# A state-space block rebuilt chunk by chunk ahead of a six-layer attention stack

## What is computed

```python
h = _layernorm(x) * (1 + ca) + sa                     # ca, sa, ga from silu(c) @ wmod
x1 = h * rsqrt(mean(h * h) + EPS) * norm_w
skip = x1 @ skip_w.T                                  # 128 -> E = 256
u = silu(causal_conv(x1 @ in_w.T, conv_w) + conv_b)   # 4 taps, per channel
delta = softplus(u @ Wd1.T @ Wd2_w.T + Wd2_b)
Bm, Cm = u @ WB.T, u @ WC.T                           # N = 16 states
# scan over positions, for each of 256 channels and 16 states:
#   H = exp(delta * A) * H + delta * u * B ;  y = sum_n H * C
y = (y + u * W_D) * silu(skip)
x = x + ga * (h + y @ out_w.T)
h2 = _layernorm(x) * (1 + cb) + sb                    # goes into the attention stack
x = x + gb * six_layers(h2)                           # q,k,v projection, rotary tables, windows of 32, FFN
```

## Time and profile before

| | us |
|---|---|
| median of 3 runs | 2322.53 (2317.49 to 2326.46) |
| the profiled execution | 2319.96 |
| its span, first to last instruction | 2318.0 |
| PE busy | 1991.3 (86%) |
| DVE busy | 1698.9 (73%) |
| ACT busy | 1470.9 (63%) |
| POOL busy | 1239.8 (53%) |

### The profile page before, as it was taken

One profiled execution on the slowest core, in us unless ns is written; L12 is line 12 of the kernel. 1 busy time (PEld: TensorE's weight loads), 2 busy tenths in 40 slices (PEclk: granted clock), 3 DMA queues, 4 the chain that ended last, 5 costly groups with the idle time before them and its releaser, 6 DMA issues. The chain is left out here.

```text
span 2318.0 us, 85232 instructions
## 1 busy us (share of the span) xinstructions
PE 1991.3 (86%) x32884; PEld 1450.5 (63%) x32884; DVE 1698.9 (73%) x3114; ACT 1470.9 (63%) x4554; POOL 1239.8 (53%) x1362
## 2 busy tenths in 40 slices
PE   4546566499989999999999999999999999999997
PEld 2212122398677697676876867857769768687672
DVE  6579897598587696775876867858669677686673
ACT  2443232397677696676767867767669667686772
POOL 3046664576475375574554854647537557455450
PEclk7779899699999999999999999999999999999998
DMA  1022120411112111121111221111211111111110
GB/s 35 3 81 72 63 72 0 146 41 41 32 42 72 38 42 37 36 79 31 43 37 31 51 70 36 40 32 42 71 38 42 37 36 43 32 44 29 25 31 18
DMA packets 147573, 103.90 MB, mean 45 GB/s; under 512 B 15778, under 2 KB 140256, under 8 KB 145504
## 3 DMA queue, kind: packets, MB, share of 16 engines
q1 hardware_dynamic: 147184, 98.55, 15.3%
HBM read 47.79 MB, written 1.18 MB: 21 GB/s over the span
## 5 line engine op out<-in xcount | busy, mean ns | idle before, releaser
L947 ACT ACTIVATE PR<-ps,MN 128x64 f32<-128x64 f32 x1536 | 354.9, 313 | 389.3 <-DVE MN L1069 388.8
L1198 POOL TENSOR_TENSOR QK<-PC,PS 128x256 f32<-128x256 f32 x384 | 278.6, 725 | 600.1 <-DVE PS L1108 543.0
L1203 POOL TENSOR_TENSOR QK<-QK,RN 128x512 f32<-128x512 f32 x384 | 401.6, 1046 | 161.1 <-ACT RN L937 133.0
L821 PE MATMUL ps<-W,XS 128*128 128x256 f32 x1536 | 399.3, 383 | 19.2 <-DMA W<-in_Wqkv 18.9
L793 PE MATMUL ps<-V,PT 64*32 64x65 f32 x12288 | 301.7, 220 | 8.6 <-ACT PT L988 5.1
L821 PEld LDWEIGHTS ps<-W,XS 128*128 128x128 f32 x1536 | 264.4, 192 | 41.4 <-DMA W<-in_Wqkv 20.5
L807 PE MATMUL ps<-ident,QK 128*128 128x128 f32 x1536 | 253.2, 287 | 35.8 <-POOL QK L1203 33.5
L1199 POOL TENSOR_TENSOR QK<-PC,PS 128x256 f32<-128x256 f32 x384 | 278.9, 726 | 0.0
L1092 DVE TENSOR_REDUCE SS<-SQ 128x8 f32<-128x512 f32 x384 | 259.3, 675 | 16.4 <-ACT SQ L979 16.4
L793 PEld LDWEIGHTS ps<-V,PT 64*32 64x32 f32 x12288 | 257.4, 105 | 18.7 <-ACT PT L988 9.2
L1069 DVE TENSOR_REDUCE MN<-ps 128x4 f32<-128x256 f32 x384 | 161.1, 419 | 142.2 <-PE ps L774 140.0
(11 more groups left out here) (142 smaller groups left out, 3447.4 us busy)
## 6 DMA issues: line engine op xcount, KB each, us to landing
V<-V SPq DMA_DIRECT2D x384, 97.5 KB, 2.2
scr<-B_rows SPq DMA_DIRECT2D x32, 512.0 KB, 3.6
V<-V SPq DMA_DIRECT2D x288, 32.5 KB, 1.9
W<-in_Wqkv SPq DMA_DIRECT2D x48, 192.0 KB, 2.9
TC<-in_tcos SPq DMA_DIRECT2D x6, 1024.0 KB, 5.9
TS<-in_tsin SPq DMA_DIRECT2D x6, 1024.0 KB, 8.4
WO<-in_Wo SPq DMA_DIRECT2D x6, 512.0 KB, 4.7
W<-in_W SPq DMA_DIRECT2D x6, 341.0 KB, 3.4
```

What stands on the lines that cost most here:

```text
L821: mm = nc.tensor.matmul(ps[:, par, k * 2 * P:(k + 1) * 2 * P], cols[k], W[:, i, 0:2, :].rearrange("p t m -> p (t m)"), start=True, stop=True)
L947: e = nc.scalar.activation(PR[:, m % 2, h, slot * DH:(slot + 1) * DH], ps[:, 4 + h, slot * DH:(slot + 1) * DH], ACT.Exp, scale=-1.0, bias= ...
L1198: nc.gpsimd.tensor_tensor(QK[:, par, :, 0:hd], PC[:, par, :, 0:hd], PS[:, par, :, hd:DH], ALU.add)
L1203: nc.gpsimd.tensor_tensor(QK[:, par, :, :], QK[:, par, :, :], bcast_last(RN[:, par, :], DH), ALU.mult).then_inc(qk, 1)
```

## The change

Nothing of the arithmetic of the attention stack changes. In `mamba_block`:
- x comes in four DMAs, the weights behind three semaphores. The stages are interleaved by chunk in an order written out by hand in every stream.
- Each inverse root is exp(-0.5 * ln(v)) on ACT (`inverse`, `level`) in place of a square root on ACT and a reciprocal on DVE. Table sets are loaded by hand: six loads (silu, exp and ln, in turn).
- The convolution is folded into the input projection: POOL multiplies the input weights by the norm weights and by each tap (`w_tap`), and PE adds up four fp32 matmuls with `XN` shifted by the tap. 32 matmuls of 512 columns take the place of 8, and the 16 DVE steps are gone. The silu takes its input from PSUM.
- The joint projection's output is copied once, 96 rows (`MID`). The C row is spread by two fp32 matmuls whose stationary operand is one column of `ident`, repeated; `BCS`, `SEL` and their DVE and POOL work are gone. In PE's stream `spread(n+1)` stands between the two halves of `state(n)`, in place of after them; the loop over n is written out.
- Exp and ln of the softplus go over 1024 columns at a time; U is POOL's.
- The gates of batch 0 stand between drives of batch 1. Output projection, residual and second norm go chunk by chunk; the residual goes straight to `XRES`, the modulation writes `XS` directly (ACT the upper half, POOL the lower).
- Tables, the first layer's `W`, scales and mask are loaded in the first block: the tables and `W` (3.5 MB) on SP behind the second `spill` and ahead of the fetches of n = 4 and on. POOL scales the tables in 16 pieces between drives of batch 1; `transformer_block` starts without them.

Its core:

```diff
+            def spill(b):
+                sp.wait_ge(mid, 2 * b + 2)
+                half = slice(b * L, (b + 1) * L)
+                sp.dma_start(B_rows[:, half], MID[DDELTA:DDELTA + N, half]).then_inc(b_out[b], 16)
+
+            spill(0)
+            sp.wait_ge(b_out[0], 16)
             for n in range(4):
                 fetch(0, n, n)
+            spill(1)
+            sp.wait_ge(b_out[1], 16)
+            sp.dma_start(TC[0][:], d["tcos"]).then_inc(ld_tab, 16)
+            sp.dma_start(TS[0][:], d["tsin"]).then_inc(ld_tab, 16)
+            for t in range(3):
+                sp.dma_start(W[:, :, t, :], d["Wqkv"][0, :, t * INNER:(t + 1) * INNER]
+                             .rearrange("p (i m) -> p i m", i=PAIRS)).then_inc(ld_w0, 16)
...
+            def conv(c, h, bank):
+                pe.wait_ge(xn, c + 1)
+                for tap in range(DCONV):
+                    mm = nc.tensor.matmul(ps[:, bank, :], w_tap[:, tap, h * P:(h + 1) * P], xn_cols(c, tap),
+                                          start=(tap == 0), stop=(tap == DCONV - 1))
+                mm.then_inc(conv_ps, 1)
+
+            def skips(c, h, bank):
+                nc.tensor.matmul(ps[:, bank, :], w_skip[:, h * P:(h + 1) * P], xn_cols(c),
+                                 start=True, stop=True).then_inc(skip_ps, 1)
...
                                       start=True, stop=True)
             mm.then_inc(s_mod, 1)
-            pe.wait_ge(s_const, 1)
-            layer_norm(s_xt, mean_ps, cen, sq, var_ps, std)
-
+            for c in range(2):
+                var(c)
+                turn(c + 2)
+                mean(c + 2)
+                square(c)
+            var(2)
+            pe.wait_ge(s_taps, 2)
             pe.wait_ge(s_mod_sb, 1)
-            for c in range(NCH):
-                wait(pe, r_sq, c + 1)
...
+            conv(0, 0, 6)
+            square(2)
+            var(3)
+            conv(0, 1, 7)
+            square(3)
+            pe.wait_ge(s_xt, NCH)
+            conv(1, 0, 0)
+            conv(1, 1, 1)
+            pe.wait_ge(cen, NCH)
+            pe.wait_ge(ld_w, 80)
+            cat(0, 2)
+            pe.wait_ge(lnv, NCH)
+            skips(0, 0, 3)
+            skips(0, 1, 4)
+            pe.wait_ge(r_ln, NCH)
+            cat(1, 5)
+            skips(1, 0, 6)
+            skips(1, 1, 7)
+            rate(0, 0, 0)
+            rate(0, 1, 1)
+            pe.wait_ge(skip, 1)
+            conv(2, 0, 2)
+            conv(2, 1, 3)
+            pe.wait_ge(skip, 2)
+            rate(1, 0, 4)
+            rate(1, 1, 5)
+            pe.wait_ge(skip, 4)
+            conv(3, 0, 6)
+            conv(3, 1, 7)
+            pe.wait_ge(sp_abs, 2)
+            pe.wait_ge(relu_d, 2)
+            cat(2, 0)
+            skips(2, 0, 1)
+            skips(2, 1, 2)
+            cat(3, 3)
...
+            def spread(b, n):
+                wait(pe, hc, (b * N + n) * HALVES)
+                row = ident[DDELTA:DDELTA + 2 * N, DDELTA + N + n:DDELTA + N + n + 1].to_broadcast([2 * N, P])
                 for k in range(2):
-                    mm = nc.tensor.matmul(ps[:, bank + k, :], SEL[:, row, :],
-                                          BCS[:, b * L + k * CH:b * L + (k + 1) * CH], start=True, stop=True)
-                return mm
-
-            def state(b, n, first=False, last=False):
-                wait(pe, hc, (b * N + n) * HALVES)
-                spread(n + N, 2, b).then_inc(c_ps, 1)
...
-                        wait(pe, y_d, b * HALVES)
-                    for k in range(2):
-                        mm = nc.tensor.matmul(ps[:, 4 + 2 * h + k, :], ident[:], HC[h][:, k * CH:(k + 1) * CH],
-                                              start=first, stop=last, skip_group_check=True)
-                    mm.then_inc(yacc, 1)
-
-            pe.wait_ge(lo, 1)
...
+            def state(b, n, h, first=False, last=False):
+                pe.wait_ge(hc, (b * N + n) * HALVES + h + 1)
+                if first:
+                    wait(pe, y_d, b * HALVES)
+                for k in range(2):
+                    mm = nc.tensor.matmul(ps[:, 4 + 2 * h + k, :], ident[:], HC[h][:, k * CH:(k + 1) * CH],
+                                          start=first, stop=last, skip_group_check=True)
+                mm.then_inc(yacc, 1)
+
             pe.wait_ge(sp_abs, NCH * HALVES)
             pe.wait_ge(relu_d, NCH * HALVES)
+            pe.wait_ge(xc, 2 * NCH)
+            spread(0, 0)
...
+            def inverse(c):
+                act.wait_ge(var_ps, c + 1)
+                nc.scalar.activation(RST[:, c, :], ps[:, 4, :], ACT.Ln, bias=epsc[:]).then_inc(lnv, 1)
+                act.wait_ge(lnv, c + 1)
+                nc.scalar.activation(RST[:, c, :], RST[:, c, :], ACT.Exp, scale=-0.5).then_inc(rstd, 1)
...
+            def soft(c, banks):
+                for h in range(HALVES):
+                    n = 2 * c + h
+                    act.wait_ge(dl_ps, n + 1)
+                    nc.scalar.activation(SOFT[:, n, :], ps[:, banks[h], :], ACT.Abs,
+                                         bias=cols[:, h, 1:2]).then_inc(sp_abs, 1)
+                act.wait_ge(sp_abs, 2 * c + 2)
+                both = SOFT[:, 2 * c:2 * c + 2, :]
+                nc.scalar.activation(both, both, ACT.Exp, scale=-1.0).then_inc(sp_exp, 1)
+                act.wait_ge(sp_exp, c + 1)
+                nc.scalar.activation(both, both, ACT.Ln, bias=1.0).then_inc(sp_ln, 1)
+
...
-                c, k = q // 4, q % 4
-                act.wait_ge(pj_ps, q + 1)
-                if k < 2:
-                    dst = XP[:, k, c // 2, DCONV - 1 + (c % 2) * CH:DCONV - 1 + (c % 2 + 1) * CH]
-                    nc.scalar.copy(dst, ps[:, q % 8, :]).then_inc(pj, 1)
-                else:
-                    nc.scalar.activation(chunk(SK[:, k - 2, :], c), ps[:, q % 8, :], ACT.Silu).then_inc(pj, 1)
-            for n in range(HALVES * B):
-                h, b = n % 2, n // 2
-                act.wait_ge(conv, HALVES * B * (DCONV - 1) + n + 1)
-                v = XC[:, h, b * L:(b + 1) * L]
-                nc.scalar.activation(v, v, ACT.Silu).then_inc(xc, 1)
+            deviation(0)
+            for c in range(NCH):
+                inverse(c)
...
-
+            def centre(c):
+                dve.wait_ge(mean_ps, c + 1)
+                nc.vector.tensor_tensor(CEN[:, c, :], chunk(XT, c), ps[:, 2 + c % 2, :], ALU.subtract).then_inc(cen, 1)
+
+            def scaled(c):
+                dve.wait_ge(rstd, c + 1)
+                dve.wait_ge(sq, c + 1)
+                nc.vector.tensor_tensor(CEN[:, c, :], CEN[:, c, :], RST[:, c, :], ALU.mult).then_inc(z, 1)
...
+            def normed(c):
+                dve.wait_ge(r_rstd, c + 1)
+                dve.wait_ge(hh, c + 1)
+                nc.vector.tensor_tensor(xn_cols(c), chunk(H1, c), RMS[:, c, :], ALU.mult).then_inc(xn, 1)
...
+            pool.wait_ge(s_fold, 1)
+            pool.wait_ge(s_pads, 2)
+            nc.gpsimd.tensor_tensor(w_tap[:], w_tap[:], w_in[:].unsqueeze(1).to_broadcast([P, DCONV, E]),
+                                    ALU.mult).then_inc(s_taps, 1)
```

More of the change, by code:

```diff
@@ new lines, in silu, with gate_in, middle @@
+            def silu(c, h, bank):
+                act.wait_ge(conv_ps, 2 * c + h + 1)
+                nc.scalar.activation(chunk(XC[:, h, :], c), ps[:, bank, :], ACT.Silu,
+                                     bias=cols[:, h, 0:1]).then_inc(xc, 1)
+            def gate_in(c, h, bank):
+                act.wait_ge(skip_ps, 2 * c + h + 1)
+                nc.scalar.activation(chunk(SK[:, h, :], c), ps[:, bank, :], ACT.Silu).then_inc(skip, 1)
+            def middle(c, bank):
+                act.wait_ge(cat_ps, c + 1)
+                nc.scalar.copy(chunk(MID, c), ps[0:DDELTA + 2 * N, bank, :]).then_inc(mid, 1)
@@ new lines, in _ @@
+            soft(0, (0, 1))
+            soft(1, (4, 5))
+            load_set(nc, act, SILU)
+            for h in range(HALVES):
+                silu(2, h, 2 + h)
+            for h in range(HALVES):
+                silu(3, h, 6 + h)
+            middle(2, 0)
+            gate_in(2, 0, 1)
+            gate_in(2, 1, 2)
+            middle(3, 3)
+            gate_in(3, 0, 4)
+            gate_in(3, 1, 5)
+            load_set(nc, act, EXP_LN)
+            soft(2, (6, 7))
+            soft(3, (4, 5))
@@ L496, in _, with residual @@
                                                    ALU.mult, ALU.add).then_inc(y_d, 1)
-            for c in range(NCH):
+            def residual(c):
                 dve.wait_ge(o_ps, c + 1)
@@ new lines, in _ @@
+            for c in range(2):
+                for h in range(HALVES):
+                    drives(c, h)
+            pool.wait_ge(u_done, 2 * HALVES)
+            for k in range(4):
+                for h in range(HALVES):
+                    drive(0, 0, k, h)
+                    if k >= 2:
+                        drives(k, h)
+            with pool.Fori(1, N // 4) as m:
+                for k in range(4):
+                    for h in range(HALVES):
```

(13 more changed lines are left out.)

620 lines of the change are left out of this document (322 added, 298 removed).

## The result

The median fell from 2320.01 us (2315.67 to 2326.46) to 2236.5 us (2234.25 to 2243.84): a ratio of 0.9643, 95% interval 0.9627 to 0.9659, 83.5 us less. The forecast was 2239 in a range of 2230 to 2260.

The account below looks back on a forecast made before the run. PE was taken to bound everything from 436 us on, a chain of work with no engine full except DVE in the scan before that; 43.4 + 3.7 + 22.2 + 14.4 = 83.7 us off gave 2239, range 2230 to 2260.

Parts of the forecast that it names:

- the scan: Scans of both batches: period stays 7.26 us, the spread at 0.43 an instruction ending 0.4 us before it is wanted.
- The way to the first scan: Kernel start to first scan: 93.1 us against 136.55, 43.4 gained; 89.3 at full clock, 105 at half clock with PE bubbles.
- square(3): Last chunk's square in the first norms: ends on PE at 39.7 us at full clock, about 47 at half; 43.5 taken.
- PE's stream: After the norms, before the first scan: 48 matmuls without a long wait, 41.1 us at full clock.
- the end chain: From the last skip matmul's landing to the first scan: gate silu, table load, softplus steps and decay, 11.6 us not hidden.
- Rival 1: Way to the first scan: PE doesn't get its matmuls done in time, first scan at 105, total 2251 us; chance 0.17.
- rival 3: Scans: PE becomes the bound through half clock or slower spread instructions, 95 us over 32 states, total 2334; chance 0.03.
- Between the batches: Change of batch: scan no longer waits for POOL's gates, second D step 1.7 us later; 3.7 us gained, bounds 1 to 5.4.
- The tail: Last scan's end to the end of the first block's work: 26.5 us against 48.7, 22.2 gained; bounds 25.5 and 32.
- The seam: Start of the attention stack: 9.5 us from W already loaded, 4.9 from tables already scaled, 14.4 gained; bounds 9.5 and 15.
- Rival 2: Attention stack's start: only the load is gained, 6 of the 14.4 us go; total 2247 with tail losses; chance 0.08.
- rival 4: Scan at n = 4: the prefetch on SP delays it; 10 us beyond the 27 us cover gives 2249; chance 0.03.

Follow-up runs that it names:

- undo_seam: Changed kernel with the tables and first layer's W loaded and scaled in the attention block again: 2251.41 us, ratio 0.9702 to the kernel before.
- two_taps: Changed kernel with two of the convolution's four taps left out: 2224.81 us, ratio 0.9584 to the kernel before.
- loads4: Changed kernel with four more table loads ahead of the third chunk's softplus: 2245.15 us, ratio 0.9661 to the kernel before.
- spread96: Changed kernel with the C row spread from all 96 rows instead of 32, in the same four instructions: 2230.09 us, ratio 0.9604 to the kernel before.
- best: Changed kernel with the 96-row spread, and batch 0's last half-1 additions ahead of batch 1's first spread: 2230.48 us, ratio 0.9595 to the kernel before.
- scale2: Changed kernel with loads kept early but POOL scaling the tables at the attention stack's start: 2242.19 us, ratio 0.9655 to the kernel before.

## Why the prediction was right

The time was right and most of its steps were; one term, the scan, was sized at nothing and costs 3 to 6 us. It is also the sign that the prediction had named for being wrong: waits of DVE for PE in the scan.

- **The way to the first scan** (43.4 of gain forecast): 42.9 in the profile, 45.0 and 43.3 in the other two. The parts: `square(3)` done at 43.6 (43.5 said), PE's stream 42.4 us (41.1 said) at full clock from 45 us on, the end chain as walked (11.3 for 11.6). The 43.5 was chosen between 39.7 and 47 for an unknown clock, and these two don't add up from the prediction's own prices: three chunks at 5.9 make 39.1 with no room for the `conv` of 3.4 between them. So that it was hit is partly luck. The clock in the norms is the likely cause of the difference from the bound: in the profile of `undo_seam`, whose way is the same, the first 45 us were granted 1.00, `square(3)` was done at 38.9 and the first scan started at 88.9, near the bound of 89.3 for full clock; at 0.92 to 0.96 the other profiles with this way have 91.2 to 94.1, though not in the order of their clocks. That PE bounds the stream, `two_taps` shows; that it isn't by much, too. Rival 1, half clock and PE bubbles up to 105, didn't come: the clock over the norms was 0.92, over the stream 1.00. The table loads cost what the trace of before says, 1.28, shown by `loads4`.
- **The reciprocals** as the cause of the old bound: shown from both sides, 34.8 taken out of before and 30.5 put into after, of 40.2 us of instructions.
- **The scan** (nothing forecast): the step that failed. "I take 0.43" for an instruction of the spread was right, and so was the slack of 0.4 us at full clock; the changed kernel's timeline has it:

```profile
125.84 1.98 PE L320 MATMUL ps<-MID,ident 32*128 32x512 f32 x4 [1.62 <-DVE scr L606]
...
128.17 1.20 DVE L606 TENSOR_TENSOR scr<-scr,ps 128x1024 f32<-128x1024 f32 x1
```

  The spread ends at 127.82, 0.35 us before the product. The term that was mis-sized is the clock: "So the period stays" took it as full because the scan of before ran at 0.95 with less PE work. More work didn't bring more clock. With 32-row operands it fell again and again, and a slack of 0.4 us doesn't carry an instruction at 0.85: DVE's products waited 10.6 us for PE, 6.5 more than before, and the batches are 5.8 us longer (1.8 and 4.0). This is rival 3 in its mechanism, a few periods of it instead of all 32 states. `spread96` takes most of the falls away and gives the batches their 114 us back; its products wait 3.8 us.
- **Between the batches** (3.7 forecast): 2.8, 3.5 and 2.7. The gates are gone from the path and the second D step is late, both as said; the wait of 2.54 is larger than the 1.7 for the spread alone, and `best` shows that the order makes it.
- **The tail** (22.2): 21.2. The order of the chunks is as walked; the clock was 0.91, where it had been 0.84 and 0.68. The last D step ends 7.9 us behind the last scan, where the walk had 6.4; ahead of it the last product waits 2.17 us for PE, whose clock was 0.66 from 336 to 341 us. Later steps give 0.5 of this back:

```profile
340.69 1.22 DVE L606 TENSOR_TENSOR scr<-scr,ps 128x1024 f32<-128x1024 f32 x1 [2.17 <-PE ps L330]
```

- **The seam** (14.4): 9.8 for the load and 5.1 in the attention stack, 14.9; undone, 14 to 18 on the chip. The scaling's part was 4.9 by the walk, 5.6 at the first rotate of `scale2` and some 7.6 from the fifth step on; from before to after the 33rd product comes 5.7 us nearer to the first projection. The 5.1 of the whole stack is smaller than the stack's scatter, so that it lies so near to 4.9 is partly luck. Rival 2, that only the load is gained, falls. The fetches of n = 4 were issued at 90.92, and no drive waits for them: rival 4 falls too.

Sum of the profile: 42.9 - 5.8 + 2.8 + 21.2 + 14.9 = 76.0, which is 2318.0 - 2242.0. Forecast less this is 7.7: 5.8 for the scan, 0.9 for the change of batch, 1.0 for the tail, 0.5 for the first piece, less 0.5 at the seam. That the median nevertheless moved by 83.5 is because the profiled execution lies 7.3 above it. The second profile of the same kernel moved by 82.2, and has 3.0 of loss in the scans and 2.4 less than forecast from the last scan to the first projection, with 1.6 more at the start and 2.5 more in the attention stack. So the hit on the median is partly luck: an overlooked loss of 3 to 6 us against scatter and small gains of the same size. No step of the prediction explains these.

## What to carry to other kernels

A long elementwise instruction between two short hops costs much of its length even on an engine that is mostly idle (30.5 us for 40.2 of reciprocals), if the idle time is the wait for that instruction's input; count it on the chain, not on the engine. When work moves onto PE, ask what slack its consumer has at half clock, and don't take a granted clock of before as the clock after. Loads that one stage waits for can be issued in an earlier one as soon as their buffers are free, if the transfers queued behind them have more slack than they take (here 10 us against 27 by the prediction; in the trace the fetches were issued 7.7 us behind the first of these loads, and nothing waited).

## What the runs showed of the hardware

- The granted clock of PE fell more often when four of a state's twelve fp32 matmul instructions had operands of 32 rows (0.81 to 0.87 in the scans of the changed kernel) than when these four filled 96 rows (0.95 to 0.98), although the 64 added rows of the stationary are zeros. The Trainium skill (TensorE: Matmul & The Clock Gate, Part 1) ties the clock to how busy PE has been; here both kernels give PE the same instructions at the same places, and the one whose clock falls has the higher busy share (88 against 79%, itself a result of the slower instructions), so what the profile calls busy isn't enough to tell the clock. Why some falls remain with 96 rows is open, and so is what in the rows matters: neither 64 rows, nor 32 rows at another place, nor other values in them were tried.
- Table loads stand back to back at 1.29 us each, without a gap before the next activation (`loads4`).
- The start of the first scan scatters by 2 us between profiles of the same kernel (91.5 to 93.6), and the attention stack by 2.4 (1874.5 to 1876.9). With the variants that leave these pieces as they are, the range is 5 us (88.9 to 94.1) and 10 us (1868.9 to 1879.1). A single profile of a kernel like this one can't place terms of that size; here eight profiles against three did it for the scans.
